# Attention layers of a graph network: the projection ahead of the spreading of scores, half of the spreading behind the first block's sums, and earlier loads of log counts

## The reference, cut to what matters

```
for l in range(W.shape[0]):                      # 3 layers
    x = relu(_gat_layer(x, src, dst, W[l], att_src[l], att_dst[l], bias[l]))

def _gat_layer(x, src, dst, W, a_src, a_dst, b):
    h = (x @ W).reshape(N, H, C)
    alpha_s = einsum('nhc,hc->nh', h, a_src)     # score of a node as a source
    alpha_d = einsum('nhc,hc->nh', h, a_dst)     # score of a node as a destination
    e = leaky_relu(alpha_s[src] + alpha_d[dst], 0.2)
    m = segment_max(e, dst)
    ex = exp(e - m[dst])
    alpha = ex / (segment_sum(ex, dst)[dst] + 1e-16)
    return segment_sum(h[src] * alpha[:, :, None], dst) + b
```

## Time and profile before

| | us |
|---|---|
| median of 3 runs | 5892.55 (5889.69 to 5895.90) |
| the profiled execution's own time | 5916.56 |
| its span | 5914.7 |
| layer 0, from its first instruction to the first transpose of its main loop | 1932.03 to 1966.07 |
| layer 1, the same | 2630.04 to 2697.69 |
| layer 2, the same | 3357.37 to 3424.70 |
| PE busy, share of the span | 3519.7 (60%) |
| ACT busy, share of the span | 2631.4 (44%) |

### The profile page before, as it was taken

One profiled execution on the slowest core, in us unless ns is written; L12 is line 12 of the kernel. 1 busy time (PEld: TensorE's weight loads), 2 busy tenths in 40 slices (PEclk: granted clock), 3 DMA queues, 4 the chain that ended last, 5 costly groups with the idle time before them and its releaser, 6 DMA issues. The chain is left out here.

```text
span 5914.7 us, 68105 instructions
## 1 busy us (share of the span) xinstructions
PE 3519.7 (60%) x25247; PEld 2223.5 (38%) x25248; DVE 3123.2 (53%) x3383; ACT 2631.4 (44%) x4143; POOL 3880.3 (66%) x3309
## 2 busy tenths in 40 slices
PE   3211111221034699987999879997958782576764
PEld 2211111111034455554555445554533330454542
DVE  3544555554379555535555355555569993333323
ACT  1000000000023688887888778885059892222211
POOL 1888888888883667756776567774020687777772
PEclk7555555555566899998999989998979996777766
DMA  8222222222289789847997479975642342332222
GB/s 294 19 18 19 19 19 8 1 1 0 9 274 348 170 187 189 168 86 160 191 196 153 78 167 197 190 156 126 213 164 79 107 129 72 110 81 74 76 53 24
DMA packets 427191, 683.75 MB, mean 116 GB/s; under 512 B 177678, under 2 KB 272397, under 8 KB 422768
## 3 DMA queue, kind: packets, MB, share of 16 engines
q0 software_dynamic: 236096, 287.22, 32.3%
q1 hardware_dynamic: 172432, 350.48, 17.7%
q10 hardware_dynamic: 18336, 41.70, 2.0%
HBM read 540.73 MB, written 138.43 MB: 115 GB/s over the span
## 5 line engine op out<-in xcount | busy, mean ns | idle before, releaser
L330 POOL DMA_INDIRECT counts<-plcell_add,plcell_slot x806 | 1254.3, 1556 | 389.3 <-issue 223.9
L1675 POOL DMA_INDIRECT emxg<-xtab,emsrc x856 | 945.0, 1104 | 452.8 <-issue 259.7
L714 ACT ACT_TABLE_LOAD x1 | 1.3, 1283 | 1617.8 <-PE mtps L702 1617.8
L377 PE MATMUL plpsR<-plpiece,plbefore 128*128 128x500 bf16 (+1 forms) x81 | 47.1, 581 | 822.2 <-DVE plranked L507 809.0
L422 DVE TENSOR_REDUCE plnlow<-plsame 128x13 f32<-128x1664 bf16 x62 | 117.1, 1888 | 671.6 <-DMA counts<-plcell_add,plcell_slot 671.5
L1759 PE MATMUL dotbanks<-emmsg,emsame 128*128 128x96 f32 x1712 | 311.4, 340 | 242.8 <-DVE emsame L1939 235.3
L1161 ACT ACTIVATE ga0prob<-ga0psE,ga0src_fifth 128x512 f32<-128x512 f32 (+1 forms) x700 | 407.8, 680 | 82.3 <-PE ga0psE L1252 79.7
L1161 ACT ACTIVATE ga2prob<-ga2psE,ga2src_fifth 128x512 f32<-128x512 f32 (+1 forms) x700 | 408.3, 683 | 80.0 <-PE ga2psE L1252 77.0
L1161 ACT ACTIVATE ga1prob<-ga1psE,ga1src_fifth 128x512 f32<-128x512 f32 (+1 forms) x700 | 407.4, 678 | 77.9 <-PE ga1psE L1252 75.2
L1252 PE MATMUL ga0psE<-ident,ga0logit 128*128 128x128 f32 x2500 | 393.4, 288 | 60.1 <-DMA ga0logit<-log_counts 38.0
L1252 PE MATMUL ga2psE<-ident,ga2logit 128*128 128x128 f32 x2500 | 395.4, 289 | 56.6 <-DMA ga2logit<-log_counts 32.8
(11 more groups left out here) (403 smaller groups left out, 8598.2 us busy)
## 6 DMA issues: line engine op xcount, KB each, us to landing
ga0logit<-log_counts POOLq DMA_DIRECT2D x88, 512.0 KB
ga1logit<-log_counts POOLq DMA_DIRECT2D x88, 512.0 KB
ga2logit<-log_counts POOLq DMA_DIRECT2D x88, 512.0 KB
counts<-plzeros SPq DMA_DIRECT2D x32, 1250.0 KB, 32.7
mthalf<-counts SPq DMA_DIRECT2D x50, 800.0 KB
log_counts<-mtlogs SPq DMA_DIRECT2D x25, 1600.0 KB
ginhalf<-counts SPq DMA_DIRECT2D x50, 800.0 KB
dotlogs<-log_counts ACTq DMA_DIRECT2D x25, 1600.0 KB
```

The lines of the kernel that those rows point to most:

```text
L330: nc.gpsimd.indirect_dma_start(counts[w][:, :], bass.IndirectOffsetOnAxis(ap=cell_slot[:, g % 2, j:j + 1], axis=0), cell_add[:, g % 2, j:j ...
L377: nc.tensor.matmul(psR[:, f // RANK_BANK, 0:k * BINS], before[:], piece[:, n % 2, f:f + k, :].rearrange("p t b -> p (t b)"), start=True, s ...
L714: nc.scalar.activation(logs[:, n % OUTS, q, :], ps[:, u % 3, 0:BW], ACT.Ln, bias=tiny[:, 0:1], scale=math.e).then_inc(log_made, 1)
L1675: nc.gpsimd.indirect_dma_start(xg[:, h, t, :], None, xtab[:, :], bass.IndirectOffsetOnAxis(ap=src[:, g, t:t + 1], axis=0)).then_inc(gather ...
```

## The change

- In layers 1 and 2 the projection goes ahead of the rows, on PE and on ACT.
- The rows are divided. On PE four stand behind the projection (ahead of the four transposes of L1192), sixteen behind those transposes, and the last twelve behind the first block's sums. On ACT the first sixteen copies stand ahead of the exponential of `place`, the other sixteen behind it, ahead of the first `add_bias`.
- `place` moves from the buffers of `prob` to those of `logit`, in all three layers, because `xT` is still read when it is written.
- New waits: DVE, before the first `clamp`, for 16 rows kept; DVE, before preparing run 4, for all 32; PE, before the first multiplication into `psO`, for all 32. The wait of PE for all rows before L1192 is gone.
- The four first loads of `mask` get the due times -0.989 to -0.986, behind the first two loads of `joins` and ahead of the third, in all three layers.

The diff, without context that it leaves unchanged:

```diff
-        place = prob[:, :, :].rearrange("p k c -> p (k c)")[...
+        place = logit[:, :, :, :].rearrange("p l q c -> p (l q c)")[...
+        HALF_ROWS = len(row_chunks) // 2
...
             if n < M_BUFS:
-                loads.append((-1 + (n + 9) / 100, 1, ("mask", j, c, q, 0)))
+                loads.append((-1 + (J_BUFS - 1) / 100 + (n + 1) / 1000, 1, ("mask", j, c, q, 0)))
...
                 columns(0)
+                if project:
+                    dve.wait_ge(row_kept, HALF_ROWS)
                 for r in range(AHEAD):
...
+                    if project and r + AHEAD == HEADS:
+                        dve.wait_ge(row_kept, len(row_chunks))
...
@@ scalar
-                    for n, (h, c) in enumerate(row_chunks):
-                        act.wait_ge(row_ready, n + 1)
-                        nc.scalar.activation(src_row[:, h, c:c + RC], psO[:, n % HEADS, 0:RC], ACT.Copy, scale=1.0 - SLOPE).then_inc(row_kept, 1)
                     for n, (t, k) in enumerate(turn_groups):
                         act.wait_ge(projected, n + 1)
...
+                def keep_row(n):
+
+                    h, c = row_chunks[n]
+                    act.wait_ge(row_ready, n + 1)
+                    nc.scalar.activation(src_row[:, h, c:c + RC], psO[:, n % HEADS, 0:RC], ACT.Copy, scale=1.0 - SLOPE).then_inc(row_kept, 1)
+
+                if project:
+                    for n in range(HALF_ROWS):
+                        keep_row(n)
                 act.wait_ge(weight_placed, 1)
                 nc.scalar.activation(weight[:]..., place, ACT.Exp).then_inc(weight_made, 1)
+                if project:
+                    for n in range(HALF_ROWS, len(row_chunks)):
+                        keep_row(n)
...
@@ tensor
-                    for n, (h, c) in enumerate(row_chunks):
-                        if n >= HEADS:
-                            pe.wait_ge(row_kept, n - HEADS + 1)
-                        nc.tensor.matmul(psO[:, n % HEADS, 0:RC], wext[:, D + h:D + h + 1].to_broadcast([D, P]), xT[:, c:c + RC], start=True, stop=True).then_inc(row_ready, 1)
                     for n, (t, k) in enumerate(turn_groups):
...
-                    pe.wait_ge(row_kept, len(row_chunks))
+                def spread_row(n):
+
+                    h, c = row_chunks[n]
+                    if n >= HEADS:
+                        pe.wait_ge(row_kept, n - HEADS + 1)
+                    nc.tensor.matmul(psO[:, n % HEADS, 0:RC], ...).then_inc(row_ready, 1)
+
+                if project:
+                    for n in range(HEADS):
+                        spread_row(n)
                     pe.wait_ge(kept, len(turn_groups))
...
                 last.then_inc(high_turned, 1)
+                if project:
+                    for n in range(HEADS, HALF_ROWS + HEADS):
+                        spread_row(n)
                 pe.wait_ge(high_steps, 1)
                 pe.wait_ge(weight_made, 1)
...
                 for n in range(BLOCK_TILES[0] * NT):
                     sum_tops(0, n)
+                if project:
+                    for n in range(HALF_ROWS + HEADS, len(row_chunks)):
+                        spread_row(n)
...
+                    if project and v == FOUR - 1:
+                        pe.wait_ge(row_kept, len(row_chunks))
                     pe.wait_ge(exp_ready, v + 1)
```

More of the change, by code:

```diff
@@ L905, in gat_attend @@
         psT = psX[:].rearrange("p (q h c) -> p q h c", h=HEADS, c=VW)
-        place = prob[:, :, :].rearrange("p k c -> p (k c)")[:, 0:NT * HEADS * WINDOWS].rearrange("p (t w) -> p t w", w=WINDOWS)
+        place = logit[:, :, :, :].rearrange("p l q c -> p (l q c)")[:, 0:NT * HEADS * WINDOWS].rearrange("p (t w) -> p t w", w=WINDOWS)
         scatter, scatter_steps = edge_scatter(nc, ctx, a, edges, tag + "s", *LAYER_GROUPS[layer])
@@ L1186, in _ @@
                         last.then_inc(projected, 1)
-                    pe.wait_ge(row_kept, len(row_chunks))
+                def spread_row(n):
+                    h, c = row_chunks[n]
+                    if n >= HEADS:
+                        pe.wait_ge(row_kept, n - HEADS + 1)
+                    nc.tensor.matmul(psO[:, n % HEADS, 0:RC], wext[:, D + h:D + h + 1].to_broadcast([D, P]), xT[:, c:c + RC], start=True, stop=True).then_inc(row_ready, 1)
+                if project:
+                    for n in range(HEADS):
+                        spread_row(n)
                     pe.wait_ge(kept, len(turn_groups))
```

## The result

The kernel after takes 5861.74 us (median of 6 runs, 5845.11 to 5869.04), the kernel before, run beside it, 5900.0 (5889.69 to 5909.18). The ratio is 0.9936 [0.9923, 0.9949]: some 38 us are gained (30 to 45), where 43.3 were forecast. The profiled execution of after took 5863.81 us, its span 5862.1.

The account below looks back on a forecast made before the run. Serial preludes of layers 1 and 2, one engine working while others stand, were taken as the bound. 2 x 20.9 + 1.5 (layer 0) = 43.3 us, off 5892.55, gave 5849; own range 5845 to 5857, wider 5842 to 5862.

Parts of the forecast that it names:

- the two covers: Layers 1 and 2: sixteen rows under the making of `place`, costing 0.1 us; twelve behind the sums, ending 8.06 later.
- cold sums: Layers 1 and 2, first block: sums still at the slow clock end at 28.6 us, not 27.3; lower gain bound 20.4.
- a load of the estimated 3.4 us: POOL's 590 KB load by the skill's formula: would land ahead of DVE; layer 0 gains 4.1 us, 46.3 in all.
- Rival 1: Rows at 1.2 GHz: last twelve slow, gain 27 us (chance 0.07); all slow, gain 2 us (chance 0.03).
- Rival 3: Prelude cover fails (ACT copies slip behind `place`) or masks make nothing faster: gain 36 to 38 us; chance 0.06.
- Rival 4: Main loops lose clock as PE no longer rests 12 us ahead; gain gone at 2.2%, 5908 us at 3%; chance 0.02.
- Later runs have two runs' time in hand: Main loops of layers 1 and 2: runs after the second have slack, so no further lateness was priced.
- the second run: Layers 1 and 2: POOL's second accumulating load lands at S + 20.1 (S: sums' end), making this run 0.8 us later.
- own range: Whole kernel: the forecast's own range, 5845 to 5857 us around 5849.
- the wider one: Whole kernel: 5842 to 5862 us, taking in forecast, rivals 2 (more gain, up to 47 us) and 3, and run scatter.
- the start value: Whole kernel: the median before, 5892.55 us, from which the gain of 43.3 us was taken.

Follow-up runs that it names:

- uncovered: The kernel after with all 32 rows directly behind the projection on PE, all copies ahead of the exponential of `place`; ratio to before 0.9983.
- none_late: The kernel after with the last twelve rows ahead of the first block's sums instead of behind them; one time, 5879.71 us.
- reorder_alone: The kernel after with the old due times of the four first mask loads, so only the order is new; ratio to before 0.9932.
- again_2: The kernel after unaltered, measured a third time on another occasion; 5867.3 us, ratio to before 0.9938.
- before_again: The kernel before, unaltered, run again for a second profile; one time, 5901.43 us.

## Why the prediction was right in its steps and wrong in the sum

**The prelude came out as forecast.** Behind the projection's start: four transposes at 8.34 (forecast 8.4), the sums' end at 26.9 (27.3), `add_bias` 8.55 behind the sums (8.9), directly behind the last copy, PE's start at 39.5 (40.3). Sixteen rows fit under `place`: ACT's sixteenth copy ends at 2640.23, `place` at 2640.34, and the exponential starts at 2640.36. The sums start warm. Layer 0 gained 1.6 (1.5), its load 6.15 us undisturbed (6.0 taken, between 4.45 and 7.5). To the loop's start I forecast 2 x 21.2 + 1.5 = 43.9; 45.5 were measured. uncovered and none_late confirm the two covers one by one, 0.67 us a row. Two workings of the prediction were slightly off, without weight for its sum: cold sums would end at 28.5, not 28.6, and a load of the estimated 3.4 us would land at 1962.0 in layer 0, behind DVE's 1961.6 and not ahead of it.

**Rival 1, rows at half clock, didn't happen.** The twelve rows ran at 1.00, 0.67 us apiece, and so did the others (24 records in 8.28 us, 32 in 10.91). The rule of the Trainium skill that I had set beside it ("TensorE: Matmul & The Clock Gate", section "A second HAM failure mode: psum-queue depth-cycling") doesn't show itself here: the rows still cycle through four banks, now in three pieces, at the full 2.4 GHz.

**Rival 3 named the gain, 36 to 38 us, but not the reason.** The cover held, and layer 0 gained.

**Rival 4, slower loops, was wrong in its mechanism.** The clock of the whole loops stayed (0.96 and 0.97), though PE rested less ahead of them. The first blocks of layers 1 and 2 did become longer, by some 8 us in all, but from a queue; where the clock had a part, some 1.3 us per block, it fell behind waits inside the block.

**The step that failed is "Later runs have two runs' time in hand".** I followed POOL's queue to its second accumulating load, priced the second run at 0.8 us per layer, and took the rest as covered. The slack was read from the order in which DVE prepares runs; POOL's queue also holds another stage's scatter steps, and the fourth load stands behind 11 us of them. The hand was 3 us at most in before (issued at 11.6 to 13.2, landed some 6 to 8 later, needed at 20.4), and a third load that is 3 to 3.5 us later used it up. The term was 0.8 per layer, of which all but 0.3 is the later start of the loop (43.9 to that start, 43.3 in the sum); the first blocks lost about 4. With that the sum is 45.5 - 8 = 37.5, close to what was measured (37 to 38, each with 8 us either way). The rows for it stood in the trace of before: the timeline of POOL behind the loop's start.

**The runs scatter more than I had counted.** I allowed 3 us either way. The six runs of after span 24 us, and the median of before was 5893 to 5907 on the other occasions, where I had started from 5892.55. The time, 5861.74, lies outside the own range of 5845 to 5857, and just inside the wider one (5842 to 5862). Of the 12.7 us by which 5849 was missed, 7.4 are the start value (5900.0 beside the kernel after) and 5.3 the gain. That the 38 us gained still lie inside the sum's bounds of 36.2 to 47.4 is in part luck: the preludes gave 1.6 more than forecast, the loops took some 7 more. The part of the program that the change leaves alone (all but preludes and loops) took 3788 to 3801 us in the profiles of all kernels here. A ratio against runs of before on the same chip is the measure; its interval here is 0.13% either way, 8 us.

## What to carry to other kernels

When a prelude is shortened, follow every in-order queue that feeds the loop until its loads have as much slack as before, and past any work of another stage that was placed into the queue: here a third load that was 3 to 3.5 us late cost about 4 us per loop, of which about 1 was the slower clock of the run behind a wait. What stands in a queue only because it was idle is best put where that queue still is idle after the change. And cover is worth its whole length while the covering engine's next step ends ahead of the covered one: sixteen of 28 rows under a 9.35 us stretch cost nothing, the next twelve cost 0.67 us each.

## What the runs showed of the hardware that I had not expected

**An accumulating load's time depends on what else moves.** For the first such load of a loop (590 KB), from issue to PE's start: 5.9 to 6.3 us with no mask loads beside it, 7.4 to 7.8 beside four, and once, in layer 1 of reorder_alone, 9.8 beside four. The formula of the Trainium skill ("DMA: Bandwidth & Descriptors", section "Anatomy of one DMA - SWDGE (gpsimd) path") would give an estimated 3.4; the undisturbed load takes nearly twice that, and the measurement decides.

**Four mask loads and POOL's load were slow in one layer, and running rows alone don't make them so.** The view by stretches (columns as above, the last two the DMA share and GB/s), 5 us from 1.4 us behind the first mask load's issue. reorder_alone, layer 1, with rows running:

```profile
2657.90:2662.90 5.00, 5.00 (x16) 2.81 (x16) 2.61 (x7) 3.72 (x8) 0.99 (x1) 1.00 0.85 289
```

The same kernel, layer 2, rows running too:

```profile
3372.10:3377.10 5.00, 5.00 (x17) 2.81 (x16) 2.60 (x7) 3.76 (x8) 0.97 (x1) 1.00 1.01 406
```

And before, layer 1, no rows running:

```profile
2687.00:2692.00 5.00, 0.00 (x0) 0.00 (x0) 3.24 (x8) 1.76 (x2) 0.99 (x1) 0.77 1.01 404
```

With rows the DMA engines moved 289 GB/s in one layer and 406 in the other, without them 404; the third mask load landed 9.6, 6.3 and 6.1 us after its issue. What made the first slow was not found.

**A POOL copy stands still beside a DVE instruction with two large inputs.** In again_2 the copy of L818 took 1.75 us, begun at 3392.61 within DVE's L1072 (3392.55 to 3393.97); in before_again the same copy took 0.53. The Trainium skill, "GPSIMD Engine Reference", section "1. Specifications", says that the two share their access to SBUF and get in each other's way when DVE reads two operands there, as L1072 does; these rows agree, 1.2 us for one copy. So do all profiles here: 235 such copies began within a SCALAR_TENSOR_TENSOR of DVE, and none ended less than 0.38 us behind it. It is one of the reasons for a fourth load later than the 3.5 us by which the third was late.
